# One FFN product moved from the loop into the tail, half products put beside two transposes, and the last product evicted and stored in halves

## The reference

```python
def ffn(x, weight, bias):            # both sides quantized in blocks of 32 along K
    xq, xs = mx_quantize(x)          # scale = max|block| / 7.5; nearest of 63 FP6 values
    wq, ws = mx_quantize(weight)
    return (xq * xs) @ (wq * ws).T + bias

def attn(X, Wq, Wk, Wv, W_G, W_O):   # 8 heads of 128, S = 2048
    q, k, v = heads(X @ Wq), heads(X @ Wk), heads(X @ Wv)
    scores = q @ k.T / sqrt(128)     # times gamma_h ** (n - m) for n >= m, else 0
    ret = groupnorm_per_head((scores * decay) @ v)
    return silu(X @ W_G) * ret @ W_O

x = x + 0.5 * ffn(layernorm(x), w, bias)
x = x + attn(layernorm(x), ...)
x = x + 0.5 * ffn(layernorm(x), w, bias)
```

## Time and profile before

| | |
|---|---|
| median of 3 runs | 484.29 us (484.23 to 484.36) |
| the profiled execution's own time | 484.67 us |
| its span (first to last instruction, slowest core) | 482.8 us |
| spans of the 8 cores | 479.5 to 482.8 us |
| TensorE busy | 432.3 us, 90% of the span |
| VectorE busy | 342.6 us, 71% |
| GpSimd busy | 256.4 us, 53% |
| ScalarE busy | 190.5 us, 39% |
| DMA, mean | 113 GB/s, 54.47 MB |

### The profile page before, as it was taken

The page is one execution under the profiler, slowest core; times in us unless marked ns, Lnnn a source line. Parts: engine busy times, 40 slices in busy tenths (PEclk is TensorE's granted clock), DMA queues, the critical chain, the costliest instruction groups (busy, mean ns, idle before and its releaser), DMA issues.

```text
span 482.8 us, 8182 instructions; the slowest of 8 cores (479.5 to 482.8 us)
## 1 busy us (share of the span) xinstructions
PE 432.3 (90%) x2410; PEld 215.5 (45%) x2456; DVE 342.6 (71%) x656; ACT 190.5 (39%) x270; POOL 256.4 (53%) x328
## 2 busy tenths in 40 slices
PE   0226799999998999999999999999999999999894
PEld 0113354545543535454545445454545454555442
DVE  3886866477888859687786868586947466756782
ACT  1547265236442071607061533426152534614400
POOL 0888765325477554655647464647451624436243
PEclk9999899999999999999999999999999999999999
DMA  7999999974363393635343533645340524233143
GB/s 200 309 182 182 189 157 183 155 116 87 89 110 67 94 208 92 110 67 143 75 133 67 153 68 88 88 88 88 87 81 12 107 45 85 47 67 65 44 153 131
DMA packets 99451, 54.47 MB, mean 113 GB/s; under 512 B 88784, under 2 KB 89040, under 8 KB 99408
## 3 DMA queue, kind: packets, MB, share of 16 engines
q1 hardware_dynamic: 93984, 43.43, 39.5%
q0 software_dynamic: 5280, 10.49, 14.9%
q10 hardware_dynamic: 144, 0.03, 0.0%
HBM read 34.28 MB, written 8.39 MB: 88 GB/s over the span
## 4 chain that ended last, share of the span: by engine, by line
PE 72%; DVE 12%; issue 6%; ACT 3%; DMA 3%; POOL 2%; SPq 1%; DVEq 1%; ACTq 0%; POOLq 0%
PE p L818 64%; DVE p L419 2%; DVE arena L434 2%; PE p L928 2%; DMA arena<-arena 2%; PE pstate L908 1%; PE p L859 1%; DVE arena L444 1%; DMA arena<-wf 1%; PE p L863 1%; PE p L847 1%; ACT arena L709 1%; ACT arena L681 1%; PE pstate L872 1%; DVE arena L522 1%
## 5 line engine op out<-in xcount | busy, mean ns | idle before, releaser
L818 PE MATMUL p<-arena 128*128 128x512 bf16 x1715 | 383.2, 379 | 8.1 <-ACT arena L709 2.7
L818 PEld LDWEIGHTS p<-arena 128*128 128x128 bf16 x1760 | 169.6, 98 | 206.8 <-issue 10.6
L434 DVE BATCH_NORM_STATS2 arena<-arena 128x6 f32<-128x512 f32 x96 | 66.5, 692 | 9.9 <-DVE arena L436 2.2
L669 ACT ACTIVATE arena<-arena 128x1024 bf16<-128x1024 f32 x16 | 19.9, 1243 | 129.1 <-POOL arena L1072 129.1
L1112 POOL TENSOR_TENSOR arena<-arena 128x1024 bf16<-128x1024 fp8e4 x16 | 34.3, 2144 | 46.9 <-DVE arena L449 46.9
L681 ACT ACTIVATE arena<-p,arena 128x128 bf16<-128x128 f32 x128 | 46.4, 473 | 19.2 <-POOL arena L1085 19.2
L444 DVE TENSOR_REDUCE arena<-arena 128x32 f32<-128x1024 f32 x29 | 35.3, 1216 | 19.3 <-ACT arena L660 10.8
L513 DVE TENSOR_TENSOR arena<-p,arena 128x1024 bf16<-128x1024 f32 x16 | 19.6, 1223 | 41.0 <-PE p L818 40.5
L908 PE MATMUL pstate<-arena 128*128 128x128 bf16 x168 | 16.4, 261 | 34.3 <-POOL arena L1048 27.5
L1105 POOL TENSOR_TENSOR arena<-arena 128x1024 bf16<-128x1024 fp8e4 x16 | 30.5, 1909 | 29.3 <-DVE arena L449 26.3
L449 DVE SCALAR_TENSOR_TENSOR arena<-arena 128x1024 fp8e4<-128x1024 f32 x29 | 37.3, 1285 | 3.4 <-DVE arena L448 0.5
(11 more groups left out here) (52 smaller groups left out, 397.1 us busy)
## 6 DMA issues: line engine op xcount, KB each, us to landing
arena<-x SPq DMA_DIRECT2D x16, 512.0 KB, 5.3
out<-arena SPq DMA_DIRECT2D x16, 512.0 KB, 2.8
arena<-wf SPq DMA_DIRECT2D x8, 512.0 KB, 11.5
arena<-wk POOLq DMA_DIRECT2D x2, 1024.0 KB, 19.9
arena<-wq POOLq DMA_DIRECT2D x2, 1024.0 KB, 31.5
arena<-wg POOLq DMA_DIRECT2D x2, 1024.0 KB, 40.0
arena<-wv POOLq DMA_DIRECT2D x2, 1024.0 KB, 41.2
arena<-wo POOLq DMA_DIRECT2D x2, 1024.0 KB, 34.0
```

Of the source, the lines that this page charges most:

```text
L434: step(e.bn_stats(bn_ln[:, n, 6 * half:6 * half + 6], x[:, 512 * half:512 * half + 512]))
L818: last = e.matmul(pair[:, half * 512:half * 512 + 512], lhs[:, kc, :], w[:, kc, half * 512:half * 512 + 512], start=(kc == 0), stop=(kc == ...
```

## The change

One f2 fewer is done in the loop: `F2_IN` is 8. Chunk 8's operand waits in an xd1 buffer, and iteration 11 gets the form that iteration 12 has. In the tail the order on TensorE is sc(15), f2(8), ret(15), wo(14), f2(9), f2(10), the turn of z(15), the first half of f2(11), wo(15), the second half of f2(11), f2(12), f2(13), the first half of f2(14), the turn of xd2(15), the second half of f2(14), then f2(15) in two halves that are each signalled (`t_last`), evicted (`v_last`) and stored by themselves. FFN 14 uses pair 1 and FFN 15 pair 0. On VectorE zmul(15) stands before ev2(10), and ev2(11) before q2(15), with ev2(12) behind it. SyncE has store(8) and store(9) between the loop and the last xdt2. GpSimd's list stays as it was.

```diff
-F2_IN = 9
+F2_IN = 8
...
-        if i == LATE - 1:
+        if F2_IN + 3 <= i < LATE:
...
-    order += [("sc", 15, 1), ("f2", 9, 2), ("ret", 15, 1), ("wo", 14, 0), ("f2", 10, 2),
-              ("f2", 11, 0), ("wo", 15, 1), ("f2", 12, 2), ("f2", 13, 0), ("f2", 14, 2),
-              ("f2", 15, 1)]
+    order += [("sc", 15, 1), ("f2", 8, 2), ("ret", 15, 1), ("wo", 14, 0), ("f2", 9, 2),
+              ("f2", 10, 0), ("f2", 11, 2), ("wo", 15, 1), ("f2", 12, 0), ("f2", 13, 2),
+              ("f2", 14, 1), ("f2", 15, 0)]
...
-    late_home = {9: cols(o_xc1[0]), 10: cols(o_xc1[0] + 2048), 11: cols(o_xc1[1]),
+    late_home = {8: cols(o_xd1[0]), 9: cols(o_xc1[0]), 10: cols(o_xc1[0] + 2048), 11: cols(o_xc1[1]),
...
             if 1 <= c < F2_IN:
                 e.wait_ge(sem["t_f2"], c)
+            elif c == 8:
+
+                e.wait_ge(sem["tr_x10"], 16 * n_dma(14, X1_DMA, 2))
...
+        store(8)
         store(9)
         xdt2(NC - 2)
-        for c in range(10, NC):
+        for c in range(10, NC - 1):
             store(c)
+        for half in range(2):
+            hs = slice(512 * half, 512 * half + 512)
+            e.wait_ge(sem["v_last"], half + 1)
+            e.dma_start(out=out_v[:, NC - 1, hs], in_=x_sb[(NC - 1) % XR][:, hs]
+                        ).then_inc(sem["st_last"], 16)
         e.wait_ge(sem["st_out0"], 16 * (NC // 2))
-        e.wait_ge(sem["st_out1"], 16 * (NC // 2))
+        e.wait_ge(sem["st_out1"], 16 * (NC // 2 - 1))
+        e.wait_ge(sem["st_last"], 32)
...
-            if i >= LATE - 1:
+            if i >= F2_IN + 3:
                 evO(i - 2)
             if i < F2_IN + 3:
                 ev2(i - 3)
             gn(i - 1)
             if i == STEADY:
                 st2(i + 1)
-            if i >= LATE - 1:
+            if i >= F2_IN + 3:
                 st3(i - 2)
-            if i < LATE - 1:
+            else:
                 evO(i - 2)
...
-        ev2(9)
+        ev2(8)
         gn(NC - 1)
         evO(NC - 2)
         st3(NC - 2)
+        ev2(9)
+        zmul(NC - 1)
         ev2(10)
-        zmul(NC - 1)
         q2(NC - 2)
-        ev2(11)
         evO(NC - 1)
         st3(NC - 1)
+        ev2(11)
+        q2(NC - 1)
         ev2(12)
-        q2(NC - 1)
         ev2(13)
         ev2(14)
-        ev2(15)
+
+        e.wait_ge(sem["g_b2"], NC)
+        for half in range(2):
+            hs = slice(512 * half, 512 * half + 512)
+            e.wait_ge(sem["t_last"], half + 1)
+            e.tensor_tensor(x_sb[(NC - 1) % XR][:, hs], pair_of("f2", NC - 1)[:, hs],
+                            x_sb[(NC - 1) % XR][:, hs], ALU.add
+                            ).then_inc(sem["v_last"], 1)
...
+        def f2_half(c, half):
+            e.wait_ge(sem["tr_x2"], 16 * (c + 1))
+            pair = emptied("f2", c)
+            for kc in range(KC):
+                last = e.matmul(pair[:, half * 512:half * 512 + 512], xdt2_at(c)[:, kc, :],
+                                wdt_sb[:, kc, half * 512:half * 512 + 512],
+                                start=(kc == 0), stop=(kc == KC - 1),
+                                skip_group_check=True)
+            if half == 1:
+                last.then_inc(sem["t_f2"], 1)
...
         sc(NC - 1)
-        f2(9)
+        f2(8)
         ret(NC - 1)
         wo(NC - 2)
+        f2(9)
         f2(10)
-        f2(11)
         e.wait_ge(sem["s_Sc"], NC - 1)
         e.wait_ge(sem["v_z"], NC)
         turn("z%d" % Z_PE, z_sb)
+
+        f2_half(11, 0)
         wo(NC - 1)
+        f2_half(11, 1)
         f2(12)
         f2(13)
-        f2(14)
+        f2_half(14, 0)
         e.wait_ge(sem["g_xd2"], NC)
         turn("y%d" % X2_PE, xd2_sb)
-        f2(NC - 1)
+        f2_half(14, 1)
+        e.wait_ge(sem["s_tb"], TURN_NO["y%d" % X2_PE] + 1)
+        pair = emptied("f2", NC - 1)
+        for half in range(2):
+            for kc in range(KC):
+                last = e.matmul(pair[:, half * 512:half * 512 + 512],
+                                xdt2_at(NC - 1)[:, kc, :],
+                                wdt_sb[:, kc, half * 512:half * 512 + 512],
+                                start=(kc == 0), stop=(kc == KC - 1),
+                                skip_group_check=True)
+            last.then_inc(sem["t_last"], 1)
```

More of the change, by code:

```diff
@@ L42 @@
        "ld_ident", "tr_x10", "tr_x11", "tr_t0", "tr_t1", "tr_k", "tr_q",
-       "tr_z", "tr_x2", "st_out0", "st_out1",
+       "tr_z", "tr_x2", "st_out0", "st_out1", "st_last",
        "v_self", "v_wy", "v_st1", "v_st2", "v_st3", "v_q1", "v_q2", "v_ev1",
@@ L50 @@
        "t_f1", "t_f2", "t_sc", "t_ret", "t_upd", "t_wo", "t_k", "t_q", "t_v",
-       "t_g", "t_tb"])
+       "t_g", "t_tb", "t_last", "v_last"])
 class Tally:
@@ L180, in build_program @@
     y82_sb = f8at(take(1024), D)
-    xd1_sb = [bfat(take(2048), D) for _ in range(2)]
+    o_xd1 = [take(2048) for _ in range(2)]
+    xd1_sb = [bfat(o, D) for o in o_xd1]
     o_xd2 = take(2048)
@@ L1188, in prog_gpsimd @@
                 smG(i - 1)
[L1189 to L1192, removed]
+            sm3(i - 2)
             if i + 5 < NC:
```

## The result

The changed kernel takes 481.68 us, median of 5 runs (480.90 to 482.92), against 484.29 (484.20 to 484.54) beside it: 2.6 us less, ratio 0.9944 with the interval [0.9927, 0.9962]. Two more groups of runs gave 481.18 against 484.53 (0.9936 [0.9916, 0.9957]) and 481.97 against 484.55 (0.9947 [0.9934, 0.9959]). The forecast was 480.8, so 3.5 us less. The direction and the range hold. The gain is small, but every interval is clear of 1; it is 2.6, 3.4 and 2.6 us in the three groups, 0.1 to 0.9 less than forecast. Both kernels scatter: in the first group the changed one over 2.0 us and the one before over 0.3, in the second the changed one over 1.2 and the one before over 3.2.

What follows compares the result with a forecast made beforehand. TensorE, busy 19.89 of 20 us in the loop, was taken as the bound, with waits only in the tail. -1.51 - 1.51 + 0.62 - 0.54 - 0.55 = -3.49 gave 481.18, or 480.8 on the median's scale; range 479.9 to 482.1 us.

Steps and rivals of the forecast that it cites:

- wait before v(11): Iteration 11: v waits for q's eviction from pair 2, behind a late group norm; +0.62 us, bounds 0 and 0.96.
- two turns covered: Tail: a half product behind the z turn and one behind the y turn each cover ScalarE's copy; -1.51 us each.
- last eviction: End of tail: the first half's eviction runs beside the second half's matmuls, so 1.23 becomes 0.69; -0.54 us.
- last store: End of span: the last store moves half the bytes; -0.55 us, between 0 and 0.65.
- Rival A: Iteration 11: no stall at v(11), as q's eviction has slack there; 480.2 us, chance 0.12.
- the thin slacks: Tail, wo(15) to y turn: evO(15) has 1.0 us spare, f2(13) 0.15 us after ev2(11).
- Rivals C: Tail: VectorE late for evO(15) beyond its spare 1.0 us, ev2(10) waiting ahead of q2(14); 1 us more gives 481.8, chance 0.05.
- D: Tail turns: a half product waits for a pair or operand, the 1.51 stays; 482.3 for one, 483.8 both, chance 0.04.
- rival B: Last store: a half-size store ends no sooner, 2 KB rows taking as long as 4 KB; 481.4 us, chance 0.06.
- part 1: Loop: f2(8) leaves iteration 11 and comes behind sc(15); by itself zero, but a 0.62 us stall before v(11).
- the prediction's own sign: Stated test: wrong if TensorE waits elsewhere in iterations 11 to 15, y turn exceeds 14.5 us after wo(15), or clock falls in tail.
- rival E: Iterations 11 to 15: pair 2's late hand-over recurs, five waits of x us; 485.2 us at x = 1.0, chance 0.05.

Runs made afterwards that it cites:

- no-fill: Changed kernel with f2(11) and f2(14) whole again, no halves beside the two turns; 482.89 us in one execution, sc(15) to the end 43.14 to 43.45 us.
- two last-product runs: Changed kernel with last product evicted and stored in one step (482.28 us), or evicted in halves but stored in one DMA (481.16 us); one execution each.

## Why the prediction was right, and where it was too good

| step | forecast | measured on an undisturbed core |
|---|---|---|
| wait before v(11) | +0.62 | +0.65 |
| wait before v(12) | 0 | +0.39 |
| two turns covered | -3.02 | -3.02 (both 1.35 gone, 14.31 against 14.32 between) |
| last eviction | -0.54 | -0.54 |
| last store | -0.55 | -0.62 (0.6 by the run with one store) |
| sum | -3.49 | -3.2 (sc(10) to sc(15): 102.40 to 99.96; to the end: 41.5 to 40.7) |
| transposes late | 0 | 0, and +0.3 to +2.1 on 1 to 5 of 8 cores |

**Right, with their reasons.** That pair 2's hand-over would hold TensorE in iteration 11, and by how much, was read from the lateness of one VectorE step in two like iterations (2.11 against 1.49). The run with q evicted first shows that it was that wait. Rival A is out. The tail's bookkeeping held to a few hundredths, the thin slacks too: evO(15) idled 1.02 us before it started where 1.0 was forecast (461.59 in the rows), the y turn came 14.31 us after wo(15), and taking the halves out cost 2.5 us. Rivals C and D are out. The halved store saved 0.62 of the 0.65 that halving the moving time allows, so rival B is out. The Trainium skill (DMA: Bandwidth & Descriptors, "Anatomy of one DMA") gives 0.60 by the bytes, as an estimate, which is as near; that section describes DMAs that GpSimd issues, while this store is SyncE's, and its sum for 512 KB, 2.0 + 1.2 = 3.2 us as an estimate, is more than the 2.6 to landing that the profile with one store shows.

**The step that failed** is in part 1. By the prediction's own sign (TensorE waiting elsewhere in iterations 11 to 15) it was wrong there, though the time came out in the range; the range had room for a whole store and a late evO(15), not for this, so that it held is luck in part. The step reads "Iterations 12 to 15 keep their form and order", from which I took that they keep their time. Two things don't follow from form and order. First, the order of VectorE's list is kept, but taking three instructions (ev2(8) and its waits) out of iteration 11 moved the end of an instruction block from behind a 0.69 us step to behind a 0.02 us one, in a chain that the earlier trace rows had shown to be without slack. It cost 0.39 us on every core (the run with three instructions more). Second, I took a transpose's landing as the median of 3.0 and gave wo(9) 3.9 us of slack, but didn't do the same sum for wo(13) and sc(15), which have 1.0 and 0.6. They had much the same in the kernel before, 0.9 and 0.6; what the change moved is the fetches. The loop is shorter by 2.4 us there while the fetches come later by 4 to 8, so that one fetch now stands 2.7 us before or 1.3 us behind the issue of z(13)'s transpose, by chance, and the next one 1 to 2 us behind that of q(15)'s or past its landing. A core then takes 0.3 to 2.1 us more. Over the six profiles whose loop is the changed kernel's (three of it, and those of the no-fill and the two last-product runs) 12 of 48 cores were disturbed.

**The other sign, rival E,** was the right place with the wrong persistence. The wait was met again in iteration 12, as it said, with 0.39 us, but by a cause of its own, and not in 13 to 15 (0.1 in 13 and in 14, as before).

What stays open is what decides between a fetch at 78 and one at 82 us after sc(10) in the same program. Both occur in one execution; of 48 cores of the changed kernel's loop, none lay between 79.0 and 82.0. That it depends on which wait TensorE's sequencer stands at when the block is used up is only an argument.

## What to carry to other kernels

When an order is shortened, redo the slack of every wait that lies behind the shortened place, with the worst landing seen and not the median, above all for a product that follows a transpose by DMA within 4 to 5 us. A difference in lateness between two iterations of like form prices a new wait well before anything is built. And an instruction removed anywhere moves the blocks in which the rest is fetched: a microsecond's change in a chain without slack may be that, and a few fulfilled waits at the start of a list are a cheap test for it.

## What the hardware showed that I had not expected

- TensorE's instructions come in packets of 16 KB on queue q8, about every 20 us in the loop, each holding one DMA engine for 0.9 to 2.1 us. Over all profiles, from 330 us on, 323 transposes of 128 x 1024 bf16 had such a packet begin 0.8 to 2.2 us behind their issue, and landed after 3.6 to 5.1 us; the 2038 with no packet near landed after 3.0 to 3.4. A store of 256 KB that met one landed after 3.6 instead of about 2.3.
- VectorE shows a gap of 0.40 to 0.42 us between two of its own instructions, with the semaphore long up, at recorded instructions 700 and 1084 (384 = 3 x 128 apart) where a short one stands before it. Behind a 0.69 us step nothing is seen of it: in the kernel before, and with three instructions more, the gap at 1084 is 0.04.
- The clock did not matter to the change: 1.00 from sc(10) to the last product, on both sides. It matters to the metric, by its fall to 0.50 early in the kernel. sc(10) comes at 334.0 to 341.8 us over all profiles; the latest is on a core with 6.8 us of it.
